# Expert tiles of 512 and 256 slots in place of 512 alone, in an attention and mixture-of-experts layer

## What is computed

```python
rh = gelu(x @ rW1 + rb1)
probs = softmax(rh @ rW2 + rb2)
weights, indices = top_k(probs, 2)
for e in range(4):
    xi = x * token_mask[..., e:e + 1]
    h = gelu(xi @ We1[e] + be1[e])
    yo = h @ We2[e] + be2[e]
    out = out + yo * combine_w[..., e:e + 1]
```

## Time and profile before

| what | us |
|---|---|
| median of 3 runs | 2059.73 |
| lowest and highest | 2054.78, 2060.18 |
| the profiled execution | 2075.05 |
| its span | 2073.3 |
| PE busy in the span | 2006.5 |
| DVE busy | 1647.4 |
| ACT busy | 1403.4 |
| POOL busy | 393.8 |

### The profile page before, as it was taken

One profiled execution on the slowest core, in us unless ns is written; L12 is line 12 of the kernel. 1 busy time (PEld: TensorE's weight loads), 2 busy tenths in 40 slices (PEclk: granted clock), 3 DMA queues, 4 the chain that ended last, 5 costly groups with the idle time before them and its releaser, 6 DMA issues. The chain is left out here.

```text
span 2073.3 us, 48468 instructions
## 1 busy us (share of the span) xinstructions
PE 2006.5 (97%) x16588; PEld 1077.1 (52%) x16588; DVE 1647.4 (79%) x2007; ACT 1403.4 (68%) x2502; POOL 393.8 (19%) x461
## 2 busy tenths in 40 slices
PE   7999999999999999999999999998998899999997
PEld 4543333333333333333333333334876799999996
DVE  6788999999999999999999999970445555665564
ACT  3348888888888888888888888887554322222221
POOL 1360010010001000100100010010054433333333
PEclk9999999999999999999999999999999999999998
DMA  7934354335334533543453355320125567776671
GB/s 264 242 78 90 74 119 93 71 87 120 79 72 99 115 72 74 121 91 71 87 120 79 72 105 109 71 61 25 57 100 219 213 236 267 260 255 237 244 261 52
DMA packets 102092, 267.69 MB, mean 129 GB/s; under 512 B 22894, under 2 KB 45936, under 8 KB 95344
## 3 DMA queue, kind: packets, MB, share of 16 engines
q1 hardware_dynamic: 91648, 241.25, 44.0%
q0 software_dynamic: 10368, 25.45, 3.5%
HBM read 212.87 MB, written 74.20 MB: 138 GB/s over the span
## 5 line engine op out<-in xcount | busy, mean ns | idle before, releaser
L588 DVE TENSOR_REDUCE part_max<-psum_attend 128x1 f32<-128x1024 f32 x1024 | 1241.9, 1222 | 59.4 <-PE psum_attend L710 47.1
L643 ACT ACTIVATE probs<-psum_attend 128x512 f32<-128x512 f32 x2048 | 1111.1, 596 | 153.2 <-PE psum_attend L723 84.3
L723 PE MATMUL psum_attend<-score_q,score_k 50*128 50x512 f32 x2048 | 748.6, 448 | 2.9 <-DMA max_k<-qk_pieces 1.7
L710 PE MATMUL psum_attend<-max_k,max_q 48*128 48x512 f32 x2048 | 741.3, 451 | 0.8 <-DVE part_max L588 0.8
L735 PE MATMUL psum_attend<-probs,v_ones 128*32 128x256 f32 x8192 | 657.2, 393 | 9.4 <-ACT heads_sb L658 9.0
L723 PEld LDWEIGHTS psum_attend<-score_q,score_k 50*128 50x128 f32 x2048 | 308.3, 185 | 409.5 <-ACT probs L643 392.9
L735 PEld LDWEIGHTS psum_attend<-probs,v_ones 128*32 128x32 f32 x8192 | 162.4, 108 | 382.6 <-issue 200.8
L710 PEld LDWEIGHTS psum_attend<-max_k,max_q 48*128 48x128 f32 x2048 | 295.5, 186 | 13.8 <-issue 7.5
L1152 ACT ACTIVATE x_sb<-psum_route,x_sb 128x512 f32<-128x512 f32 x152 | 104.8, 690 | 285.7 <-PE psum_route L1513 248.9
L1532 PE MATMUL psum_route<-w,h_hi 128*128 128x256 f32 x1216 | 217.8, 278 | 0.0
L1532 PEld LDWEIGHTS psum_route<-w,h_hi 128*128 128x128 f32 x1216 | 195.9, 189 | 14.4 <-issue 1.1
(11 more groups left out here) (171 smaller groups left out, 1508.8 us busy)
## 6 DMA issues: line engine op xcount, KB each, us to landing
w<-w_split SPq DMA_DIRECT2D x38, 2048.0 KB
max_q<-qk_pieces SPq DMA_DIRECT2D x192, 128.0 KB, 7.4
score_k<-qk_pieces SPq DMA_DIRECT2D x192, 128.0 KB, 4.6
xs<-in_pads SPq DMA_DIRECT2D x33, 528.0 KB, 5.7
qk_pieces<-pieces SPq DMA_DIRECT2D x32, 512.0 KB, 4.8
w_split<-w_pair SPq DMA_DIRECT2D x32, 512.0 KB, 6.4
max_k<-qk_pieces SPq DMA_DIRECT2D x192, 64.0 KB, 7.5
score_q<-qk_pieces SPq DMA_DIRECT2D x192, 64.0 KB, 2.2
```

What stands on the lines that cost most here:

```text
L588: nc.vector.tensor_reduce(part_max[:, t, p:p + 1], ps_m[p].rearrange("q b f -> q (b f)"), axis=AXIS.X, op=ALU.max).then_inc(m_read, 1)
L643: nc.scalar.activation(probs[kb % 2][:, chunk * BLOCK:(chunk + 1) * BLOCK], bank_of(at), ACT.Exp, scale=float(HD) ** -0.5).then_inc(exp_do ...
L710: last = nc.tensor.matmul(ps_m[p][:, h, :], max_q[u][rows, t * P:(t + 1) * P], max_k[u][rows, p * BLOCK:(p + 1) * BLOCK], start=True, stop ...
L723: nc.tensor.matmul(bank_of(at), score_k[u][rows, kb * P:(kb + 1) * P], score_q[u][rows, part * BLOCK:(part + 1) * BLOCK], start=True, stop ...
```

## The change

The fixed set of tiles is now 15 of 512 slots (`PAIRS`) and 5 of 256 (`SINGLES`), 8960 slots instead of 9728. The table has a column for each; `TILE_COL` gives the order in which they run: five full ones, then five times two full ones and a half one. `list_early` is as before. `list_late` counts for each expert the pairs of halves and all halves, and lists 10 full tiles; `list_halves`, new, lists what these leave, in 5 half tiles, at block 4 of tile 1. Every engine's work on a half tile covers 2 blocks of 128 slots instead of 4 (`TILE_BT`): transposes, the columns of the hidden matmuls, the number of the output matmuls, ACT's and DVE's widths, row loads, gathers and stores. Its weights are loaded whole. `accumulate` moves from block 3 to block 5 of the next tile, and the token numbers have three buffers instead of two. The diff, cut:

```diff
-MOE_TILES = PER_TOKEN * TOKENS // SLOTS + EXPERTS - 1
+HALF_TILE = SLOTS // 2
 REGION = TOKENS
 XS_ROWS = EXPERTS * REGION + SLOTS
 GATE_AT, ID_AT, ROW = DIM, DIM + EXPERTS, DIM + 8
 CHUNK = 512
 W_CHUNKS = 2 * DIM * HIDDEN // (P * CHUNK)
-STEPS = TOKENS // SLOTS - 1
+STEPS = TOKENS // HALF_TILE
+
+HALF_TILES = PER_TOKEN * TOKENS // HALF_TILE + EXPERTS - 1
 EARLY = PER_TOKEN * SEQ // SLOTS - EXPERTS + 1
-LATE = MOE_TILES - EARLY
+SINGLES = EXPERTS + (HALF_TILES - EXPERTS) % 2
+LATE = (HALF_TILES - SINGLES) // 2 - EARLY
+PAIRS = EARLY + LATE
+MOE_TILES = PAIRS + SINGLES
+
+TILE_COL = list(range(EARLY))
+for single in range(SINGLES):
+    TILE_COL += range(EARLY + single * LATE // SINGLES, EARLY + (single + 1) * LATE // SINGLES)
+    TILE_COL.append(PAIRS + single)
+TILE_BT = [BT if col < PAIRS else BT // 2 for col in TILE_COL]
+BT_UPTO = [sum(TILE_BT[:n]) for n in range(MOE_TILES + 1)]
...
-    LAG, PS_H, H, HALVES = 2, 2, 2, 4
+    LAG, PS_H, H, HALVES, ACCUMULATE_AT = 2, 2, 2, 4, 5
...
-    token = [sb(f"token{u}", [P, BT], U32) for u in range(2)]
+    TOKEN_SETS = 3
+    token = [sb(f"token{u}", [P, BT], U32) for u in range(TOKEN_SETS)]
...
+            elif TILE_COL[i] == PAIRS:
+                sp.wait_ge(table_ready, 3)
             elif i == EARLY:
...
-            start = sp.value_load(table[0:1, 0, i:i + 1], min_val=0, max_val=EXPERTS * REGION)
-            expert = sp.value_load(table[0:1, 1, i:i + 1], min_val=0, max_val=EXPERTS - 1)
+            col, bt = TILE_COL[i], TILE_BT[i]
+            start = sp.value_load(table[0:1, 0, col:col + 1], min_val=0, max_val=EXPERTS * REGION)
+            expert = sp.value_load(table[0:1, 1, col:col + 1], min_val=0, max_val=EXPERTS - 1)
...
-            sp.dma_start(xs[u], dram["xs"][ds(start, SLOTS), :].rearrange("(t p) f -> p t f", p=P)
+            sp.dma_start(xs[u][:, 0:bt, :], dram["xs"][ds(start, bt * P), :].rearrange("(t p) f -> p t f", p=P)
...
-                pool.wait_ge(out_stored, 16 * BT * i)
+                pool.wait_ge(out_stored, 16 * BT_UPTO[i])
             if i == EARLY:
                 pool.wait_ge(residual_out[1], 16 * HALF)
-            for t in range(BT):
+            for t in range(TILE_BT[i]):
...
             u = i % 2
             pool.wait_ge(y_summed, i + 1)
-            for t in range(BT):
+            for t in range(TILE_BT[i]):
...
-        def list_tiles(first_of, first, n, taken_of):
+        def list_tiles(first_of, col, n, at_slots, slots, before_first):
...
-            if taken_of is None:
-                small(nc.vector.scalar_tensor_tensor(shift_of[:], first_of, -float(SLOTS), regions, ALU.mult, ALU.add))
-            else:
-                small(nc.vector.tensor_tensor(shift_of[:], taken_of, first_of, ALU.subtract))
-                small(nc.vector.scalar_tensor_tensor(shift_of[:], shift_of[:], float(SLOTS), regions, ALU.mult, ALU.add))
+            small(nc.vector.scalar_tensor_tensor(shift_of[:], first_of, -float(slots), regions, ALU.mult, ALU.add))
+            if before_first is not None:
+                small(nc.vector.scalar_tensor_tensor(shift_of[:], before_first, float(HALF_TILE), shift_of[:],
+                                                     ALU.mult, ALU.add))
             small(nc.vector.tensor_tensor(by, pick_of, shift_of[:].unsqueeze(1).broadcast_to(per_tile), ALU.mult))
...
+        def count_tiles(out, steps, op):
+            n = steps.shape[1]
+            per_step = [P, EXPERTS, n]
+            small(nc.vector.tensor_tensor(over[:, :, 0:n], count[:].unsqueeze(2).broadcast_to(per_step),
+                                          steps.unsqueeze(1).broadcast_to(per_step), op))
+            small(nc.vector.tensor_reduce(out, over[:, :, 0:n], axis=AXIS.X, op=ALU.add))
+
+        def take(out, tiles, first_of, n):
+
+            small(nc.vector.tensor_scalar(out, first_of, -1.0, float(n), ALU.mult, ALU.add))
+            small(nc.vector.tensor_scalar_max(out, out, 0.0))
+            small(nc.vector.tensor_tensor(out, out, tiles, ALU.min))
+
+        def list_early():
+
             small(nc.vector.tensor_tensor(count[:], free_slot[:], regions, ALU.subtract))
-            small(nc.vector.tensor_tensor(over[:], count[:].unsqueeze(2).broadcast_to(per_step),
-                                          full_tiles.unsqueeze(1).broadcast_to(per_step), op))
-            small(nc.vector.tensor_reduce(out, over[:], axis=AXIS.X, op=ALU.add))
-
-        def list_early():
-
-            count_tiles(full[:], ALU.is_ge)
+            count_tiles(full[:], even_steps, ALU.is_ge)
             sum_earlier(first_full[:], full[:])
-            list_tiles(first_full[:], 0, EARLY, None)
-            small(nc.vector.tensor_scalar(taken[:], first_full[:], -1.0, float(EARLY), ALU.mult, ALU.add))
-            small(nc.vector.tensor_scalar_max(taken[:], taken[:], 0.0))
-            small(nc.vector.tensor_tensor(taken[:], taken[:], full[:], ALU.min))
+            list_tiles(first_full[:], 0, EARLY, tile_slots, SLOTS, None)
+            take(taken[:], full[:], first_full[:], EARLY)
 
         def list_late():
-            count_tiles(tiles_of[:], ALU.is_gt)
-            small(nc.vector.scalar_tensor_tensor(tiles_of[:], tiles_of[:], 1.0, taken[:], ALU.add, ALU.subtract))
-            sum_earlier(first_tile[:], tiles_of[:])
-            list_tiles(first_tile[:], EARLY, LATE, taken[:])
+
+            small(nc.vector.tensor_tensor(count[:], free_slot[:], regions, ALU.subtract))
+            count_tiles(halves_of[:], half_steps, ALU.is_gt)
+            count_tiles(pairs_of[:], odd_steps, ALU.is_gt)
+            small(nc.vector.tensor_tensor(pairs_of[:], pairs_of[:], taken[:], ALU.subtract))
+            small(nc.vector.tensor_scalar_add(pairs_of[:, EXPERTS - 1:EXPERTS], pairs_of[:, EXPERTS - 1:EXPERTS], float(LATE)))
+            sum_earlier(first_pair[:], pairs_of[:])
+            small(nc.vector.tensor_scalar(taken[:], taken[:], 2.0, None, ALU.mult))
+            list_tiles(first_pair[:], EARLY, LATE, tile_slots, SLOTS, taken[:])
+
+        def list_halves():
+
+            take(in_pairs[:], pairs_of[:], first_pair[:], LATE)
+            small(nc.vector.scalar_tensor_tensor(taken[:], in_pairs[:], 2.0, taken[:], ALU.mult, ALU.add))
+            small(nc.vector.tensor_tensor(halves_of[:], halves_of[:], taken[:], ALU.subtract))
+            small(nc.vector.tensor_scalar_max(halves_of[:], halves_of[:], 0.0))
+            sum_earlier(first_half[:], halves_of[:])
+            list_tiles(first_half[:], PAIRS, SINGLES, half_slots, HALF_TILE, taken[:])
...
-            if i >= 2:
-                dve.wait_ge(out_stored, 16 * BT * (i - 1))
+            if i >= TOKEN_SETS:
+                dve.wait_ge(out_stored, 16 * BT_UPTO[i - TOKEN_SETS + 1])
...
-            nc.vector.tensor_copy(token[u][:], xs[u][:, :, ID_AT]).then_inc(prepared, 1)
+            nc.vector.tensor_reduce(gate[u][:, 0:bt], gates[u][:, 0:bt], axis=AXIS.X, op=ALU.add).then_inc(prep_step, 1)
+            nc.vector.tensor_copy(token[i % TOKEN_SETS][:, 0:bt], xs[u][:, 0:bt, ID_AT]).then_inc(prepared, 1)
...
-            nc.vector.tensor_copy(h_hi[m % HALVES], h[m % H]).then_inc(h_hi_ready, 1)
+            nc.vector.tensor_copy(h_hi[m % HALVES][:, 0:n], h[m % H][:, 0:n]).then_inc(h_hi_ready, 1)
             dve.wait_ge(h_hi_ready, s + 1)
-            nc.vector.tensor_tensor(h_lo[m % HALVES], h[m % H], h_hi[m % HALVES].bitcast(F32),
+            nc.vector.tensor_tensor(h_lo[m % HALVES][:, 0:n], h[m % H][:, 0:n], h_hi[m % HALVES][:, 0:n].bitcast(F32),
...
-            dve.wait_ge(gathered, 16 * BT * (i + 1))
-            nc.vector.tensor_tensor(y[u], y[u], rows[u][:], ALU.add).then_inc(y_summed, 1)
+            dve.wait_ge(gathered, 16 * BT_UPTO[i + 1])
+            nc.vector.tensor_tensor(y[u][:, 0:bt, :], y[u][:, 0:bt, :], rows[u][:, 0:bt, :], ALU.add).then_inc(y_summed, 1)
...
-                    elif m == 3:
+                    elif m == ACCUMULATE_AT:
                         accumulate(i - 1)
...
+                if i == 1 and m == LATE_TABLE:
+                    list_halves()
...
-                for t in range(BT):
+                for t in range(TILE_BT[i]):
...
-                last = nc.tensor.matmul(ps_h[m % PS_H], w[u][:, 2 * k + m // 4, c, at:at + P], xx[:, k, :],
+                last = nc.tensor.matmul(ps_h[m % PS_H][:, 0:n], w[u][:, 2 * k + m // 4, c, at:at + P], xx[:, k, 0:n],
...
-            for t in range(BT):
+            for t in range(TILE_BT[i]):
```

More of the change, by code:

```diff
@@ L936, in route_and_experts @@
     taken = sb("taken", [P, EXPERTS])
+    in_pairs = sb("in_pairs", [P, EXPERTS])
     ps_x = psum[:, 2:4, :]
@@ L1125, in split_x @@
                 act.wait_ge(h_ready, MH * (i - 1))
-            nc.scalar.activation(xT[i % 2][0], ps_x, ACT.Copy).then_inc(x_hi, 1)
+            n = TILE_BT[i] * P
+            nc.scalar.activation(xT[i % 2][0][:, :, 0:n], ps_x[:, :, 0:n], ACT.Copy).then_inc(x_hi, 1)
         for i in range(BLOCKS):
@@ L1151, in gelu @@
```

(3 more changed lines are left out.)

73 lines of the change are left out of this document (39 added, 34 removed).

## The result

| | us |
|---|---|
| changed kernel, median of 20 runs | 2069.80 (2062.13 to 2094.45) |
| kernel before, 20 runs on the same chips | 2058.63 (2053.62 to 2085.55) |
| ratio | 1.0058, 95% interval 1.0039 to 1.0077 |
| profiled execution of the changed kernel | 2062.55, span 2060.8 |

The change makes the kernel 11 us slower, with an interval of 8 to 16 us. The prediction was 2041.6 us with a range of 2028 to 2058: wrong in sign, and the time lies outside the range. The ratio leaves out the one run of 2094.45 us, which was a slow one.

What follows compares the result with a forecast made beforehand. The prediction took PE, busy 97% of the span, as the bound. Its terms -34.8 + 0.3 + 12 + 4.4 sum to -18.1 us, from a median of 2059.73 to 2041.6 us, range 2028 to 2058.

Steps and rivals of the forecast that it cites:

- PE term, -34.8 us: Expert stage: four full tiles fewer save 92.3 us, five half tiles of 11.5 us add 57.5.
- rival (5): Half tiles: a 256-column hidden matmul costs the 0.235 us of a 512-column one; 28.8 us back, 2070 us; chance 0.03.
- `list_late` and `list_halves`, +0.3: Small list instructions on DVE: four more in `list_late` cost PE 0.3 us; 21 new in `list_halves` cost 0.
- Four steps: +12 us: Full-to-half steps: DVE waits at `accumulate` for late gathers, stalling PE 3.0 us each, four times.
- the upper end of my bounds: PE's stall per full-to-half step, at most 0.3 + 5.4 + 0.8 = 6.5 us, from one late gather and store.
- Without weights the chain: Between two `accumulate`s: add, stores, gathers and landings outlast PE's work on a quiet DMA, costing PE 0.3 to 0.6 us.
- 0.2 us of slack for the x split: Full tile after a half one: split takes 3.36 us, PE wants it at 3.56; DVE waits just before pass to PE.
- 16.3 to 16.6 against 15.8: Full-full-half sequence: us of add, stores, gathers and landings against us of PE work between the two `accumulate` places.
- Rival (4), the clock: Stalls let PE's clock fall: some 2.2 us lost five times, 11 us on top, 2053 us; chance 0.04.
- Rival (3): Gathers land behind the next 2 MB of weights: 12 us stall four times, 2078 us; slower from 7.5 a step; chance 0.05.
- The tail, +4.4: Kernel end: span ends 18.5 us after PE instead of 14.1, with DVE waiting 8 to 9 us for the last gather.

Runs made afterwards that it cites:

- experiment 2: Changed kernel with weights loaded for the first two tiles only, the others computing with what lies in the buffers: 2041.5 us, ratio to before 0.9921.
- experiment 5: Kernel before with only `accumulate` moved to block 5 and three token sets, all 19 tiles full: 2064.46 us, ratio 1.0028.
- experiment 8: Changed kernel with `accumulate` at block 3 and 480 bytes of pad ahead of `h_hi`: 2023.91 us, again 2032.97; order full, half, full also tried: 2029.49, 2027.82.
- experiment 3: Changed kernel without the gathers, `accumulate` adding what its buffers hold, all weights loaded: 2028.33 us, ratio to before 0.9857.

## Why the prediction was wrong

**PE term, -34.8 us: right to 1.4 us.** 2 x 23.08 + 11.5 = 57.7 was forecast for a group without stalls and 57.95 measured on the mean, once the two faults were mended. With 11.8 us for a half tile the term is -92.3 + 59.0 = -33.3. A 256-column hidden matmul costs 0.12 us: rival (5) is out.

**`list_late` and `list_halves`, +0.3: nothing measured.** From 1605 to 1643.88 us, where both run, PE is busy all the time; the two full tiles from 1643.88 on are 46.83 us, the same as in the kernel before with 32 bytes of pad.

**"Four steps: +12 us": the step that failed.** I had the mechanism (`accumulate` at block 5 in the half tile, late stores and gathers, DVE, the x split, PE), and took 3.0 us a step, "the middle" between 0.3 and 6.5. It measured 8.1 on the mean, 32.3 us in all. Of the 8.1, 5.9 are PE's wait: twice what I took, and near the upper end of my bounds. The other 2.3 are the clock, for which this term had nothing; with it the step lies outside the bounds. Without weights the chain was to cost PE 0.3 to 0.6 us, and steps cost 1.1 to 4.2 (experiment 2, where loads of rows still meet the gathers). The upper end was built from one late gather and one late store, 5.4 and 0.8 us, and came near the sum with the wrong parts: the stores took 3.5 us more here, the issue of the gathers 0.8, and the last gather about 2. By then there was no cover left anywhere, and I had found that myself: 0.2 us of slack for the x split. Bounds that come from one row of a kernel in which the thing was covered should not be averaged; a chain that is as long as its cover on a quiet queue (16.3 to 16.6 against 15.8, by the prediction) is over it on a busy one. The Trainium skill (DMA: Bandwidth & Descriptors, section Queues, rings and completion order) has the queues take turns packet by packet; as I applied that, DVE would have waited under 1 us. The trace does not agree with what I made of it: 6.3 us.

**Rival (4), the clock: it came on top.** I gave it 4 in 100 beside the others, as if it excluded them. It follows from them: all four waits of about 6 us were followed by work at the 1.2 GHz level, 2.3 us lost each on the mean, close to the 2.2 that I had priced, though it is four times and not the five of the prediction. Rival (3) named the point from which the change loses, 7.5 us a step; the steps passed it, with 8.1, though not by the mechanism given there, a gather behind the following tile's weights. The Trainium skill (TensorE: Matmul & The Clock Gate, section Why this matters for your kernels) warns of waits between thin matmuls, and the rows at 0.50 behind these waits agree.

**The tail, +4.4: measured +2.8.** The wait for the last gather is 8.00 us, within the 8 to 9 forecast. The move causes it rather than the half tile: experiment 5 has +4.9 with full tiles alone, and at block 3 the tail is 13.9 us, as before.

**Not foreseen: the place of `h_hi`.** Some 4.7 us: 13.7 full tiles of the stretch at 0.34, and nothing for the half ones. In experiment 8 the pad gave back 3.5 us of stretch, while waits for `h_lo` in the last groups took about 1 us more. The kernels show that the tables ahead of `h_hi` change their sizes; I read nothing in it.

**The sum again.** The stretch of before was 408.0. Less 33.3, plus 4.7 for the place in memory, is 379.4; experiment 3, which has both and no stall, took 379.7. With 32.3 for the four steps that is 411.7, and 0.8 more is a wait of PE for `h_lo` near the end: 412.5. Measured were 412.8, and 0.3 us stay unnamed. With 2.8 in the tail the change costs 7.6 us in the two traces, just under the 8 to 16 of the runs' interval; where the rest lies, ahead of the stretch or in the spread of single executions, is open.

## What to carry to other kernels

Before a task is made shorter, list what hides behind its length: here a store, landing and gather chain of 16 us, fixed in time, under a tile that shrank from 23 us to 11.8. Such a chain should start as early as it can, and what waits for it should not stand right ahead of what the bounding engine needs next: in the same kernel one block number was worth 35 us (32.3 in the stretch and 3.0 in the tail). And when an engine that does the same work becomes evenly slower by a per cent or so, look at what has moved in memory before looking for a wait.
